# Four graph layers on one core: the mask of the attention scores taken out of the matrix products and put into two copies of the adjacency, of which a transfer picks one per head and tile

## The reference

```
h = relu(layernorm(x)); x = x + silu(rmsnorm((adj @ h + eps*h) @ W1 + b1)) @ W2 + b2      # layer 0
h = relu(layernorm(x)); x = x + attention from sigmoid(s1_i + s2_j) * adj, rows normed    # layer 1
# layer 2, 8 heads of 32 features, softmax over j:
scores = q @ k.T / sqrt(32) + adj * W_e[h]
scores = where(adj != 0, scores, -inf);  x = x + (softmax(scores) @ v) @ W_o.T
# layer 3, with degrees d = sum_j adj + 1e-5:
x = x + d^-0.5 * adj * d^-0.5 @ (relu(layernorm(x)) @ W3) + b3
```

## Time and profile before

| | us |
|---|---|
| median of 3 runs | 3797.84 (3796.89 to 3798.93) |
| the profiled execution, its own time | 3793.83 |
| its span, first to last instruction | 3792.0 |
| one pass of the steady loop | 115.1 |
| TensorE busy | 3595.9 |
| VectorE busy | 2623.7 |
| ScalarE busy | 2279.2 |
| GpSimd busy | 772.2 |

### The profile page before, as it was taken

How to read it: one execution, slowest core, us unless ns; L and a number is a source line. 1 busy time by engine, 2 the same in 40 slices (tenths; PEclk the granted TensorE clock), 3 DMA queues, 4 the chain that set the end, 5 groups by cost and what they waited for, 6 DMA issues and landing times.

```text
span 3792.0 us, 67268 instructions
## 1 busy us (share of the span) xinstructions
PE 3595.9 (95%) x19375; PEld 2445.7 (64%) x19596; DVE 2623.7 (69%) x6436; ACT 2279.2 (60%) x5029; POOL 772.2 (20%) x1611
## 2 busy tenths in 40 slices
PE   4899999999999999999999999999999999999997
PEld 3566666666666666666666666666666666666664
DVE  4676776666767766767767766667677667677664
ACT  2565666555666656666656665556666566666564
POOL 1122211222212222212222112222122222122210
PEclk9999999999999999999999999999999999999999
DMA  2232132322232322223321323222323222233212
GB/s 85 62 85 72 56 89 56 89 74 69 67 78 67 89 67 67 78 57 87 85 71 56 89 56 89 75 70 67 78 67 89 67 67 78 57 87 85 65 45 67
DMA packets 166936, 275.09 MB, mean 73 GB/s; under 512 B 23906, under 2 KB 59874, under 8 KB 166756
## 3 DMA queue, kind: packets, MB, share of 16 engines
q1 hardware_dynamic: 166756, 273.45, 26.7%
HBM read 122.37 MB, written 16.78 MB: 37 GB/s over the span
## 4 chain that ended last, share of the span: by engine, by line
PE 61%; issue 13%; DVE 12%; POOL 8%; ACT 5%; POOLq 0%; DMA 0%; DVEq 0%; SPq 0%; another core or an unknown queue 0%; ACTq 0%
PE turn L1213 9%; PE front L1026 7%; PE score L1203 6%; PE front L1027 6%; PE front L1028 6%; PE score L1204 4%; PE value L1228 3%; POOL small L374 3%; PE front L1056 3%; PE front L1079 3%; PE score L1177 3%; PE value L1189 3%; DVE pT L813 2%; ACT hf L500 2%; PE front L1068 2%
## 5 line engine op out<-in xcount | busy, mean ns | idle before, releaser
L588 ACT ACTIVATE prob<-prob,small 128x512 f32<-128x512 f32 x1024 | 736.1, 719 | 375.4 <-DVE small L888 373.8
L888 DVE CUSTOM_DVE_ANT_0 prob<-score,adj_sb,drv 128x512 f32<-128x512 f32 x1024 | 759.4, 747 | 224.8 <-PE score L1204 126.9
L1213 PE MATMUL turn<-ident,prob 128*128 128x128 f32 x4096 | 617.1, 276 | 14.6 <-ACT pT L597 8.7
L1213 PEld LDWEIGHTS turn<-ident,prob 128*128 128x128 f32 x4096 | 484.9, 141 | 134.8 <-issue 62.0
L597 ACT ACTIVATE pT<-turn 128x512 f32<-128x512 f32 x768 | 446.5, 584 | 144.6 <-PE turn L1213 144.6
L1203 PE MATMUL score<-qk_stack 128*128 128x512 f32 x1024 | 496.0, 488 | 31.5 <-DVE small L888 29.9
L1026 PE MATMUL front<-w_hi,s_hi 128*128 128x256 f32 x1024 | 353.0, 345 | 28.6 <-DVE x_in L792 28.6
L1204 PE MATMUL score<-unlinked,neg_mask 128*128 128x512 bf16 x803 | 313.6, 391 | 0.0
L680 DVE TENSOR_TENSOR s_lo<-front,s_hi 128x512 fp32r<-128x512 f32 x320 | 217.7, 680 | 102.7 <-ACT s_hi L486 102.6
L1027 PE MATMUL front<-w_lo,s_hi 128*128 128x256 f32 x1024 | 288.0, 281 | 0.0
L1028 PE MATMUL front<-w_hi,s_lo 128*128 128x256 f32 x1024 | 287.6, 281 | 0.0
(11 more groups left out here) (160 smaller groups left out, 7447.2 us busy)
## 6 DMA issues: line engine op xcount, KB each, us to landing
qk_stack<-qk SPq DMA_DIRECT2D x1024, 128.0 KB, 2.4
adjT_f<-in_adjT SPq DMA_DIRECT2D x32, 1024.0 KB, 5.0
adj_sb<-in_adj SPq DMA_DIRECT2D x32, 1024.0 KB, 7.9
prob<-in_adjT SPq DMA_DIRECT2D x32, 1024.0 KB, 5.4
x_new<-in_x SPq DMA_DIRECT2D x32, 512.0 KB, 3.7
out<-x_out SPq DMA_DIRECT2D x32, 512.0 KB, 3.1
pT<-in_W SPq DMA_DIRECT2D x2, 1024.0 KB
rmsw_b<-in_rmsw SPq DMA_DIRECT2D x1, 512.0 KB
```

Of the source, the lines that this page charges most:

```text
L588: act.activation(prob[:, i % 8, :], prob[:, i % 8, :], ACT.Exp, bias=nmax[:, h, n:n + 1], scale=-1.0, accum_out=prsum[:, h, n:n + 1]).then ...
L888: dve.tensor_tensor_reduce(out=prob[:, i % 8, :], in0=SB_[i % 2][:, :], in1=adj_sb[:, n, :], scale=neg_w[:, h:h + 1], scalar=3e38, op0=ALU ...
L1213: last = pe.transpose(TB[k % 2][:, tile(n)], prob[:, (4 * h + n) % 8, tile(j)], ident[:, :])
```

## The change

- The mask product, `neg_mask` and `unlinked` are gone; a score tile is one product.
- `edges` holds two copies of the adjacency, each with the far nodes set to an end: adj + 1e37 where adj is 0 (`edges_neg`), and 2 adj minus that copy, which is adj with -1e37 there. VectorE makes them in the tail, one graph ahead: `far_nodes` (one instruction of 128 x 2048), `edges_below` (four of 128 x 512), `edges_above` (four of 128 x 512), and `degree`.
- `bias` reads its tile from `edge`, a ring of three tiles. SyncE fills the ring: `pick_edges` waits until the bias three before has read its slot and copies the 128 x 512 tile (256 KB) of the copy that fits the sign of the head. The sign is read once into registers.
- `qk_stack` has three slots, so `stack` of head h waits for the scores of head h-3; stacks and picks stand in one written order on SyncE.
- The order changes: the tiles of layer 0 come two steps earlier in relation to the scores, `turn_hidden` a step later within them and behind the score; the last tile's quarters lie in steps 27 and 28, two each; the projections of q and k for heads 4 to 7 stand in steps 1 and 4 (before 0 and 3). The second half of the aggregation goes from the end of the pass behind `project_qk` of the next; `project_v(1)` goes from before the scores to step -2.
- `project_qk` of heads 0 to 3 writes the turn banks. The last product of layer 3 has a bank of its own (a front bank).
- x of the next graph lies in a part of `pT`, and its load waits for the end of the attention product.

```diff
-        unlinked = sb("unlinked", [P, NT, N], BF16)
+        edges = sb("edges", [P, 2, NT, N])
+        adj_sb, edges_neg = edges[:, 0, :, :], edges[:, 1, :, :]
+        edge = sb("edge", [P, 3, N])
-        qk_stack = sb("qk_stack", [P, 4, 2, N], F32R)
+        qk_stack = sb("qk_stack", [P, 3, 2, N], F32R)
...
-            return [(n, g + 4 - 8 * n) for n in range(NT) if 0 <= g + 4 - 8 * n < 16]
+            return [(n, g + 6 - 8 * n) for n in range(NT) if 0 <= g + 6 - 8 * n < 17]
...
-                return range(4) if u == 8 else ()
+                return (2 * u - 18, 2 * u - 17) if u in (9, 10) else ()
...
+            def pick_edges(t, i):
+                h, n = divmod(i, NT)
+                if h == 0:
+                    sp.wait_ge(edges_ready, at(t, 4, n + 1))
...
+                if i >= 3:
+                    sp.wait_ge(biased, at(t, 32, i - 2))
...
+                s = edge_slot(i)[0]
+                sp.dma_start(edge[:, s, :], edges[:, bass.ds(sign_of[h], 1), n, :].rearrange("p o n -> p (o n)")).then_inc(edge_in[s], 16)
...
+                    for i in range(3):
+                        pick_edges(t, i)
+                    stack(t, 0)
+                    stack(t, 1)
+                    pick_edges(t, 3)
+                    stack(t, 2)
+                    for i in range(4, 4 * H):
+                        pick_edges(t, i)
+                        if i >= 5 and i % 4 == 1 and i // 4 + 2 < H and i != 9:
+                            stack(t, i // 4 + 2)
+                        if i == 14:
+                            stack(t, 4)
...
-            def graph(t):
-                dve.tensor_scalar(unlinked[:, :, :], adj_sb[:, :, :], 0.0, None, ALU.is_equal).then_inc(unlinked_ready, 1)
-                dve.tensor_reduce(deg, adj_sb[:, :, :], AX.X, ALU.add).then_inc(deg_ready, 1)
+            def degree(tf):
+                dve.tensor_reduce(deg, adj_sb, AX.X, ALU.add).then_inc(deg_ready, 1)
+            def far_nodes(tf):
+                dve.tensor_scalar(edges_neg, adj_sb, 0.0, BIG, ALU.is_equal, ALU.mult).then_inc(far, 1)
+            def edges_below(tf):
+                for n in range(NT):
+                    dve.tensor_tensor(edges_neg[:, n, :], adj_sb[:, n, :], edges_neg[:, n, :], ALU.add).then_inc(edges_neg_ready, 1)
+            def edges_above(tf):
+                for n in range(NT):
+                    dve.scalar_tensor_tensor(out=adj_sb[:, n, :], in0=adj_sb[:, n, :], scalar=2.0, in1=edges_neg[:, n, :],
+                                             op0=ALU.mult, op1=ALU.subtract).then_inc(edges_ready, 1)
...
-                dve.tensor_tensor_reduce(out=prob[:, i % 8, :], in0=SB_[i % 2][:, :], in1=adj_sb[:, n, :],
+                dve.tensor_tensor_reduce(out=prob[:, i % 8, :], in0=SB_[i % 2][:, :], in1=edge[:, i % 3, :],
...
-                pe.matmul(SB_[i % 2][:, :], neg_mask[:, h, :], unlinked[:, n, :],
-                          start=False, stop=True).then_inc(sc_ps, 1)
```

170 lines of the change are left out of this document (95 added, 75 removed).

## The result

The kernel became slower, not faster: 3906.4 us median (3904.9 to 3908.2, 4 runs) against 3797.4 for the kernel before, ratio 1.029 [1.027, 1.031]. The forecast was 3680, its range ended at 3810. The profiled execution took 3904.9 us, its span is 3902.7.

The account below looks back on a forecast made before the run. TensorE's order was taken to set the time, with VectorE near in two stretches. B 0.2, C 0.3, D 4.3 and tail -1.0 gave 3.8 us a pass, 118 us over 31 passes: 3680 us, range 3560 to 3810.

Parts of the forecast that it names:

- The mask's price: Mask products on TensorE: 0.32 us each, 10.2 us a pass (at least 0.23 and 7.4).
- A: Stretch of a pass from first score to tenth, 14.8 us before; forecast 16.3, 1.5 more, given back in E.
- B: Stretch from tenth score to twenty-first, 19.5 us before; forecast VectorE-bound, about 18, then 19.3 with late picks: 0.2 saved.
- C: Stretch from twenty-first score to twenty-fifth, 11.8 us before; forecast 11.5 by TensorE's steps: 0.3 saved.
- D: Stretch from twenty-fifth score to the end of the turns, 21.7 us before; forecast 17.4: 4.3 saved.
- What the other engines need in the grid: Step summing engines' work in stretches A to D under the new order: A 16.3, B about 18, C 11.5, D 17.4 us.
- E: Stretch holding the tail with the next start, 47.3 us before; forecast 1.5 less as project_v(1) moves to A.
- The picks: Step on edge-tile transfers: landing 2.5 us after issue, bias 15 late by 1.7 behind paired stacks, 1.3 taken in B.
- The tail: VectorE's added copy operations, 5.5 to 9.6 us more work; far_nodes ahead of the update costs 1.0 us (bounds 0 and 3).
- TensorE as the limit: Rival for the whole pass: TensorE stays the limit, 9.2 us a pass saved, 3513 us; chance 0.12.
- Slower, the ring sets the pace: Rival in the grid: picks landing at 4.4 us make a pass 5 us longer, 3950 us; chance 0.15.
- The transfers eat the gain: Rival in A, B and C: late picks and stacks leave 0.3 us a pass, 3788 us (3735 to 3800); chance 0.23.

Follow-up runs that it names:

- the direct kernel: Changed kernel (new order) without picks: each bias reads the right copy in place, by this input's signs written into the program; 3836.6 us, 1.010 to the kernel before.
- old order, direct: Changed kernel with every engine's order as before the change, copies still made and read in place by written-in signs, no picks; 3782.4 us, 0.997 to the kernel before.

## Why the prediction was wrong

- **The mask's price** was mis-sized first. I took 0.32 us, 10.2 a pass. In the changed kernel the product behind a score starts just as late, with no mask between (TensorE's timeline):

```profile
1937.41 0.48 PE L1266 MATMUL score<-qk_stack 128*128 128x512 f32 x1
1937.73 0.28 PE L1088 MATMUL front<-w_hi,s_hi 128*128 128x256 f32 x1
```

  The 0.32 belong to the score. The mask's own is my lower bound, 0.23, and so 7.4 us a pass (236 us in all). And of the 7.4 the kernel kept 2.8 when the mask alone went: I forecast 4.8 in the grid, new order included.
- **A, B, C and D added up an engine's work stretch by stretch.** The step that failed is the one headed "What the other engines need in the grid". It took each stretch as long as its fuller engine, and counted too little for TensorE in C and D: it is busy 12.7 us in C (I had 11.5) and 13.5 in D up to the last turns (I reckoned with 10, for which no row stood, and with VectorE's 12.3 as the limit). VectorE's own work in D was right: 12.6 us up to the end of the last bias. But that bias ends 14.8 us into D and not at 13, since VectorE waits 3.9 us for two scores in between, and the last turns start at 15.9 and not at 14.1. In A, B and D neither engine is full; they wait in turn. "D saves 4.3 us" was the largest term; D saved 2.6, and A, B and C got 3.3, 1.4 and 0.9 us longer, where I had 1.5 longer for A (given back in E), and 0.2 and 0.3 shorter. Without picks the new order alone is 2.1 us a pass worse than the old at the same clock. So the term D rested on a sum of work where a chain of hand-overs set the pace, and taking the mask alone out gave 2.8 us a pass where the sum of TensorE's time promised 7.4.
- **The picks** land in 2.3 us (2.5 assumed), and the place (bias 15) and cause (stack pair) of the longest wait were right: 1.80 us where I expected 1.7. But it is worth only 0.5; biases 4 and 6, where I expected no wait over 0.5 us, wait for 0.77 and 0.45 and keep nearly all of it: the direct kernel is 0.4 us ahead at bias 0 (for a reason that the trace does not name) and 1.2 at bias 4. In all 1.8 us a pass instead of 1.3, by the table; the size came out near the forecast while its place did not, which is luck in part.
- **The tail** came out as forecast: 1.35 us longer from the load of the transposed adjacency to the store (36.65 against 35.3), 1.0 taken. The rule that I had quoted from the Trainium skill (page "SBUF — State Buffer", section "SBUF: two separate sides") made 0.5 of it, at a place that I had not named: the norm behind layer 1, not the addition of b2. That section also lets VectorE take the lock in its two-port modes. `far_nodes`, with one input, beside GpSimd's 1.09 and 1.99 us agrees, though no row names the mode in which it ran.
- **Start-up and the last back half** were counted at nothing. They lost 12.2 and 7.7 us. The direct kernels show what of this is the order: its first store is at 253.0 us in the new order and 243.3 in the old.
- **The rivals.** TensorE as the limit is out by the idle time. "Slower, the ring sets the pace" named 3950 and wanted a landing time of 4 us: the sign was right and the mechanism wrong, as picks land in 2.3. "The transfers eat the gain" has the right size for the picks, with a gain that was not there.

The accounting in medians, each step a measured pair: mask products -77, copies +62 (old order, direct, against the kernel before without mask), new order +54, picks +70; in all +109. The last two depend on which is taken first: picks +137 and then the new order -13 come to the same sum.

## What to carry to other kernels

Taking work from the fullest engine pays only as far as the others can follow step by step: take that work out alone first, and measure what it gives (here 77 us, where the sum of its time was over 230), before paying for its replacement. In a queue that waits in order, a transfer's own wait holds all behind it, and the wait that the profile shows at one instruction is not what its removal gives, since the next one may be just behind. When two kernels are compared by the pass, compare passes at the same granted clock, and count the others apart. Work put into VectorE's free time is free only if GpSimd has nothing on the path at that moment.

## What the runs showed of the hardware

- GpSimd's operation on 4 values a row takes 0.20 us, and up to 2.43 us beside four additions of VectorE from SBUF (in 21 of 30 passes; in nine, at the same place, 0.62); its power takes 1.02 us, and 1.99 beside one operation of VectorE with a single fp32 input.
- 1024 transfers of 256 KB inside SBUF changed neither a bias nor a score by a tenth of a microsecond where nobody waited for them.
- The sum of TensorE's idle time does not tell what clock is granted. In the kernel before (3.6 us idle a pass) it is 1.00 in every pass but the last. Without mask products (6.4 us idle) it falls in 8 of 30 passes, for 3.4 us each, and seven of the falls begin 15.7 to 16.0 us behind the store; such a pass has 0.985 and takes 113.5 instead of 112.3 us. Before each of the seven TensorE had waited 0.78, 0.17 and 0.35 us between scores, and no longer (before the one at 1836.1 us it was busy for 7.8 of 9.1 us); a pass in which nothing falls has the same three waits. The new order read directly, with 9.3 us idle a pass, has two such passes of 30. With the layer-0 tiles put back it is 0.92 to 0.96 and a pass takes 128 to 131 us. Of the two levels, 1.2 and 2.4 GHz, such a pass has some of its time at the lower one. What decides it is not shown.
